# The first layer's lookup compares on VectorE, written with a scalar operand

## The chip, the core and the metric

The kernel runs on one core of one Trainium2 chip. The metric is the device time of one execution in microseconds; medians of several executions are compared. On the core five engines work at the same time: TensorE (PE), VectorE (DVE), ScalarE (ACT), GpSimd (POOL) and SyncE (SP), which here only starts DMAs. They wait for each other through semaphores.

## What is computed

A graph network of four layers over 6250 nodes with 64 features and 200000 edges, sorted by their destination. Each layer normalizes the nodes' features (h), gathers h at each edge's source node, makes a message of it and sums the messages at the destination. The four layers differ in the message; the change concerns the first:

```python
h = jnp.maximum(_layernorm(x, axis=-1), 0.0)
msg = jnp.concatenate([h[src], edge_attr_32], axis=1)            # 64 + 32 features
agg = jax.ops.segment_sum(msg, dst, num_segments=h.shape[0])
x = x + relu(jnp.concatenate([h, agg], axis=1) @ W.T + b)
```

The second and the fourth layer have attention over the edges of a destination (a softmax of scores), the third a weighted sum.

## The kernel before

**Tiling.** The edges, padded, form 1568 tiles of 128, and four tiles are a batch: 392 batches of 512 edges. Each layer is one pass over all batches, one instruction stream per engine, written with a helper `pipeline` (L160): in step t an engine works through a list of stages, each for batch t minus the stage's lag. The first layer's pass is `sum_sweep` (L916, called as "sum0" in L1782). The second layer's pass is `score_sweep`, the third's `kept_sum_sweep`, the fourth's `attention_sweep`.

**Rows by gather.** GpSimd fetches the source nodes' rows from HBM, one indirect DMA per tile of 128 edges (L781, in `gather_stage`), so four per batch, each with 128 node numbers that lie in `idx_slots`. A ring of 8 batches of row buffers (`sum_rows`, a view of `rows`) receives them; before a batch's gathers GpSimd waits until TensorE's sum of eight batches ago is done. The other passes gather too, but the third reads stored rows.

**Rows by lookup.** One batch in eight (the fourth of a block of eight) is not gathered but looked up. For it, the one-hot matrix of source node against edge is built in 49 pieces: piece n has a one where an edge's source is node 128 n + lane. The 512 source numbers of the batch, as int16 and the same in all 128 lanes, stand in `look_lines` (a view of `pre`). VectorE compares them with the lane's node number for pieces 0 to 31 (stage `hots`, four instructions per batch, L1178), into a ring of four tiles `dve_hots` (a view of `dst_pairs`, under whose name the rows show it). ScalarE makes pieces 32 to 48 with Square and Relu (L1075, L1079). TensorE multiplies each piece with the node features, split into three bf16 parts (L1105), and VectorE sums the result into the row buffer once per block (`fill`, L1192). So 48 blocks have 32 compares each: 1536.

**The lane's node number.** `node_at` (float32, 128 lanes x 32, L300) holds 128 n + lane, made by an iota at the start (L550). `node_pairs` (int16, 128 x 32 x 2, L302) is the same number twice over, copied from it (L558).

**The rest of the pass.** VectorE's stages in their order are: `build` (L1136, a one-hot of the destinations), the first compare, `low` (L1156), the second compare, `high` (L1163), the third compare, `add` (L1146, which takes the sum of the batch six steps before from TensorE), the fourth compare, `fill`. The constant operands of `build`, `low` and `high` lie in PSUM (`iota_mark` and `lane_mark`, in a bank); the compares of `hots` have both operands in SBUF. TensorE per batch: the sum, eight float32 matrix instructions (L1097), then the lookups of six or seven pieces. SyncE loads edge data and lines once in four batches, stores 712 KB for the third layer's pass with them, and loads `look_lines` and `idx_slots` once in eight.

**The scalar form elsewhere.** The second and the fourth layer's passes have one compare per batch of 512 int16 numbers with a number per lane, bf16 out, with the scalar `window_lane` (float32, one per lane), in `hot_stage` (L861).

Of the kernel before, what the change touches and what calls it, by code (L numbers as in the profile page):

```python
# [33 lines left out]
ALU = mybir.AluOpType  # L34
# [3 lines left out]
P = 128  # L38
# [10 lines left out]
BATCH = TILES_PER_BATCH * P  # L49
# [84 lines left out]
def landed(eng, sems, b, per_use):  # L134

    ring = len(sems)
    eng.wait_ge(sems[b.slot(ring)], (b.uses(ring) + 1) * per_use)
# [100 lines left out]
def graph_layers(nc, a, out):  # L238
    ctx = contextlib.ExitStack()
    with ctx:  # L240
        def sb(name, shape, dt=F32):
            return ctx.enter_context(nc.sbuf_tensor(name, shape, dt))
# [57 lines left out]
        node_at = sb("node_at", [P, HOTS_DVE])  # L300
        lane_pair = sb("lane_pair", [P, 1, 2], BF16)
        node_pairs = sb("node_pairs", [P, HOTS_DVE, 2], I16)  # L302
# [613 lines left out]
        def sum_sweep(name):  # L916
# [4 lines left out]
            def sweep():  # L921
                with Phase(nc, name) as ph:
# [8 lines left out]
                    s_hot_dve, s_used_dve, s_square, s_hot_act, s_used_act, s_filled = (  # L931
                        ph.sem(n) for n in ("hot_dve", "used_dve", "square", "hot_act", "used_act",
                                            "filled"))
# [9 lines left out]
                    dve_hots, act_hots = hots_room[:, 0:4, :], hots_room[:, 4:6, :]  # L943
# [28 lines left out]
                    def block_of(b):  # L972
                        return b.uses(LOOK_EVERY)

                    def has_lookup(b):
                        return b.i is not None or b.off < N_BATCHES - LOOK_EVERY

                    def look_in(b):
                        return look_lines[:, b.of_group(LOOK_EVERY).slot(2), :]

                    def hots_dve(b):
                        n = HOTS_DVE // LOOK_EVERY
                        return range(n * b.slot(LOOK_EVERY), n * (b.slot(LOOK_EVERY) + 1))
# [148 lines left out]
                    def _(dve):  # L1132
# [35 lines left out]
                        def hots(b, which):  # L1168
                            if not has_lookup(b):
                                return  # L1170
                            if b.slot(LOOK_EVERY) == 0 and which == 0:
                                landed(dve, s_look, b.of_group(LOOK_EVERY), 16)
                            before = block_of(b) * HOTS_DVE
                            for n in hots_dve(b)[which:which + 1]:
                                if n >= 4 or not b.early(LOOK_EVERY):
                                    dve.wait_ge(s_used_dve, before + n - 3)
                                wide = [P, BATCH // 2, 2]
                                dve.tensor_tensor(  # L1178
                                    dve_hots[:, n % 4, :].rearrange("p (e t) -> p e t", t=2),
                                    look_in(b).rearrange("p (e t) -> p e t", t=2),  # L1180
                                    node_pairs[:, n:n + 1, :].to_broadcast(wide),
                                    ALU.is_equal).then_inc(s_hot_dve, 1)

                        def fill(b):
                            if b.slot(LOOK_EVERY) != LOOK_EVERY - 1 or not has_lookup(b):
# [12 lines left out]
                        for tiles in src_groups:  # L1198
                            value = of_tiles(normed, tiles)
                            left = parts_left.rearrange("p (j d) -> p j d", d=D)[:, 0:len(tiles), :]  # L1200
                            parts = [parts_of(tiles)[:, :, n, :] for n in range(PARTS)]
                            c.do(split(dve, c, value, left, parts))
                        hot0, hot1, hot2, hot3 = (functools.partial(hots, which=n) for n in range(4))
                        dve.wait_ge(s_marks, 2)
                        pipeline(dve, [(0, build), (6, hot0), (2, low), (6, hot1), (2, high),
# [1124 lines left out]
```

## Time and profile before

| | us |
|---|---|
| median of 3 runs | 6827.51 |
| lowest and highest | 6827.16, 6832.52 |
| the profiled execution | 6814.61 |
| its span in the profile | 6812.8 |

The profile is of one execution. In its rows a line begins with the line number of the kernel, the engine, the operation and what is written and read, by the names of the buffers. "Busy" is the time in which an engine has an instruction in work; instructions of one engine can overlap at their ends. "Idle before" is the time in which the engine was idle ahead of the group's instructions, with what ended it; "issue" there is time in which it waited for nothing that the profile shows. PEclk, or the number behind the counts in the rows by window, is TensorE's granted clock as a share of full speed.

### The profile page before, as it was taken

The numbers are of one execution on the slowest core, as the hardware profiler recorded it, in microseconds if no ns is written. First come the engines' busy times: TensorE is split into PE (matmuls) and PEld (weight loads), VectorE is DVE, ScalarE is ACT, GpSimd is POOL, SyncE is SP. The second block draws the span as 40 slices with busy tenths as digits, with TensorE's granted clock in tenths as the row PEclk, the third lists the DMA queues.
The fourth block names the chain that finished last, engine by engine and source line by source line (L and its number), as shares of the span: only waits on it lengthen the run. The fifth ranks groups of instructions, "written<-read, shape, count | busy, mean of one in ns | idle before, by whom it ended". The sixth has DMA issues, their size and how long they took to land. (4 is left out here: it accounts for less than half of the span.)

```text
span 6812.8 us, 161253 instructions
## 1 busy us (share of the span) xinstructions
PE 4834.9 (71%) x37998; PEld 3572.7 (52%) x38194; DVE 4807.6 (71%) x21264; ACT 4176.3 (61%) x11642; POOL 5060.7 (74%) x5713
## 2 busy tenths in 40 slices
PE   5777777777776666666665669998777777777774
PEld 4666767776662233322332258885555555555553
DVE  7666666666656666666666679997766666666667
ACT  4666666666625555555555569995566666666664
POOL 6777777777747777777777759994777777777774
PEclk8889888888877766677677679998777787777776
DMA  4333333333346666666666658886333333333231
GB/s 143 110 108 109 108 109 108 109 108 109 107 110 170 169 170 170 170 169 170 169 170 170 170 170 268 267 267 241 77 79 79 79 80 79 79 79 79 79 79 47
DMA packets 672779, 908.53 MB, mean 133 GB/s; under 512 B 141174, under 2 KB 429928, under 8 KB 672441
## 3 DMA queue, kind: packets, MB, share of 16 engines
q1 hardware_dynamic: 502366, 605.50, 29.0%
q0 software_dynamic: 168944, 301.30, 19.0%
q8 instruction: 42, 0.69, 0.0%
q10 hardware_dynamic: 1357, 0.47, 0.0%
q14 instruction: 70, 0.57, 0.0%
HBM read 696.57 MB, written 210.28 MB: 133 GB/s over the span
## 5 line engine op out<-in xcount | busy, mean ns | idle before, releaser
L781 POOL DMA_INDIRECT rows<-src_rows,idx_slots x1563 | 1494.9, 956 | 530.7 <-issue 475.2
L781 POOL DMA_INDIRECT rows<-rel_rows,idx_slots x1563 | 1481.9, 948 | 509.8 <-issue 447.7
L781 POOL DMA_INDIRECT rows<-node_rows,idx_slots x1371 | 1423.4, 1038 | 439.7 <-issue 410.2
L1371 PE MATMUL bank<-onehot,ones 128*128 128x512 f32 x1568 | 1235.5, 882 | 130.0 <-ACT onehot L1380 123.4
L1380 ACT ACTIVATE onehot<-ident,fresh_slots 128x128 f32<-128x128 f32 x3136 | 989.3, 386 | 35.6 <-DVE fresh_slots L1507 33.9
L1075 ACT ACTIVATE dst_pairs<-pre,minus_node 128x512 bf16<-128x512 int16 x816 | 580.6, 717 | 664.9 <-PE bank L1105 664.7
L1468 PE MATMUL bank<-w_e,edge_in 128*128 128x256 f32 x784 | 400.3, 606 | 751.4 <-DVE onehots L861 726.8
L1451 ACT ACTIVATE onehot<-onehots,exp_bias 128x512 bf16<-128x512 f32 x392 | 283.0, 722 | 936.4 <-DVE max_by_chunk L1549 889.8
L1468 PEld LDWEIGHTS bank<-w_e,edge_in 128*128 128x128 f32 x784 | 167.3, 264 | 1245.0 <-DVE onehots L861 801.5
L1105 PE MATMUL bank<-by_chunk,dst_pairs 128*128 128x192 bf16 x6144 | 725.6, 267 | 9.3 <-DVE dst_pairs L1178 9.2
L1178 DVE TENSOR_TENSOR dst_pairs<-pre,node_pairs 128x512 bf16<-128x512 int16 x1536 | 631.9, 411 | 0.0
L1105 PEld LDWEIGHTS bank<-by_chunk,dst_pairs 128*128 128x128 bf16 x6144 | 592.9, 107 | 34.7 <-DVE dst_pairs L1178 14.8
L1674 PE MATMUL bank<-rows,onehot 128*128 128x65 f32 x3136 | 539.8, 327 | 55.8 <-DVE wide_room L1767 53.8
L1492 DVE TENSOR_TENSOR pre<-bank,rows 128x256 f32<-128x256 f32 x392 | 166.0, 423 | 569.7 <-DMA rows<-src_rows,idx_slots 566.1
L1079 ACT ACTIVATE dst_pairs<-dst_pairs,ones 128x512 bf16<-128x512 bf16 x816 | 540.8, 707 | 1.6
L1674 PEld LDWEIGHTS bank<-rows,onehot 128*128 128x128 f32 x3136 | 496.8, 241 | 72.0 <-issue 61.7
L1146 DVE TENSOR_TENSOR wide_room<-bank,wide_room 96x128 f32 x392 | 111.4, 284 | 597.0 <-PE bank L1097 595.9
L1629 ACT ACTIVATE onehot<-onehots,edge_in 128x128 f32<-128x128 bf16 x1568 | 500.7, 390 | 20.0
L1299 ACT ACTIVATE onehot<-onehots,edge_scale 128x128 f32<-128x128 bf16 x1568 | 500.9, 390 | 14.6 <-DVE onehots L1354 14.5
L1690 DVE CUSTOM_DVE_ANT_0 pre<-bank,rows 128x64 f32<-128x64 f32 x1568 | 258.8, 221 | 319.8 <-DMA rows<-rel_rows,idx_slots 315.4
L1614 ACT ACTIVATE shrink<-grown 128x1 f32<-128x1 f32 x392 | 79.5, 203 | 648.7 <-DVE grown L1718 648.7
L1105 PE MATMUL bank<-wide_room,dst_pairs 128*128 128x192 bf16 x3264 | 439.7, 261 | 24.8 <-ACT dst_pairs L1079 24.7
(306 smaller groups left out, 11964.5 us busy)
## 6 DMA issues: line engine op xcount, KB each, us to landing
edge_in<-dst_line SPq DMA_DIRECT2D x392, 256.0 KB
spill<-rows SPq DMA_DIRECT2D x392, 256.0 KB
rows<-spill SPq DMA_DIRECT2D x392, 256.0 KB, 3.2
hot_rows<-rows SPq DMA_DIRECT2D x98, 712.0 KB
onehots<-hot_rows SPq DMA_DIRECT2D x196, 356.0 KB, 3.5
onehots<-src_low SPq DMA_DIRECT2D x98, 512.0 KB, 6.3
edge_in<-in_ea_l SPq DMA_DIRECT2D x98, 256.0 KB
edge_in<-in_eaT_l SPq DMA_DIRECT2D x392, 64.0 KB
```

The source lines that it names most:

```text
L781: pool.indirect_dma_start(out=to[:, b.slot(ROW_RING), g, :], out_offset=None, in_=table, in_offset=bass.IndirectOffsetOnAxis(ap=idx_slots[ ...
L1075: act.activation(act_hots[:, n % 2, :], look_in(b), ACT.Square, bias=minus_node[:, n:n + 1]).then_inc(s_square, 1)
L1079: act.activation(act_hots[:, n % 2, :], act_hots[:, n % 2, :], ACT.Relu, scale=-1.0, bias=ones[:, 0:1])\
L1105: last = pe.matmul(look_banks(b)[g // 2][:, at:at + PARTS * D], hot[:, g * P:(g + 1) * P], node_parts(j), start=(j == 0 and g % 2 == 0), s ...
L1178: dve.tensor_tensor(dve_hots[:, n % 4, :].rearrange("p (e t) -> p e t", t=2), look_in(b).rearrange("p (e t) -> p e t", t=2), node_pairs[:, ...
L1299: last = act.activation(onehot[:, b.slot(RING), g, :], plain_of(b)[:, g, :], ACT.Copy, scale=edge_scale[:, b.slot(RING), g:g + 1])
L1371: return pe.matmul(bank, ones[:, :], diag[:, b.slot(2), :, :].rearrange("p g e -> p (g e)"), start=start, stop=True)
L1380: last = act.activation(diag[:, b.slot(2), g, :], ident[:, :], ACT.Copy, scale=fresh_slots[:, b.slot(2 * RING), g:g + 1])
L1451: act.activation(exp_out, masked1[:, b.slot(2), :], ACT.Exp, bias=exp_bias[:, slot, :], accum_out=exp_sum[:, slot, :])
L1468: pe.matmul(to, edge_blocks[:, b.slot(RING), :], w1_e[:, :, :].rearrange("p g f -> p (g f)"), start=True, stop=False)
L1629: last = act.activation(weighted[:, b.slot(2), g, :], onehot_b[:, b.slot(ONEHOT_RING), g, :], ACT.Copy, scale=share[:, b.slot(RING), g:g + 1])
L1674: last = pe.matmul(summed, weighted[:, b.slot(2), g, :], rows[:, b.slot(ROW_RING), g, D:2 * D + 1], start=(g == 0), stop=(g == TILES_PER_B ...
```

## The change

The four compares of `hots` per batch were tensor-tensor instructions over pairs of elements: the numbers of `look_lines`, seen as 256 pairs, against the pair in `node_pairs`, which is read again for each of the 256. They become tensor-with-scalar instructions: the 512 numbers against one float32 scalar per lane, column n of `node_at`. Output, waits, semaphores and place in the order are the same; each engine has as many instructions as before. `node_pairs` stays in the program and is read by nobody.

```diff
                             for n in hots_dve(b)[which:which + 1]:
                                 if n >= 4 or not b.early(LOOK_EVERY):
                                     dve.wait_ge(s_used_dve, before + n - 3)
-                                wide = [P, BATCH // 2, 2]
-                                dve.tensor_tensor(
-                                    dve_hots[:, n % 4, :].rearrange("p (e t) -> p e t", t=2),
-                                    look_in(b).rearrange("p (e t) -> p e t", t=2),
-                                    node_pairs[:, n:n + 1, :].to_broadcast(wide),
-                                    ALU.is_equal).then_inc(s_hot_dve, 1)
+                                dve.tensor_scalar(dve_hots[:, n % 4, :], look_in(b),
+                                                  node_at[:, n:n + 1], None, ALU.is_equal)\
+                                   .then_inc(s_hot_dve, 1)
```

## Rows read from the trace of the kernel before

**Rows 1.** The page's head: the span, and each engine's busy time, share, instructions.

```profile
span 6812.8 us, 161253 instructions
PE 4834.9 (71%) x37998; PEld 3572.7 (52%) x38194; DVE 4807.6 (71%) x21264; ACT 4176.3 (61%) x11642; POOL 5060.7 (74%) x5713
```

**Rows 2.** Costliest groups, whole execution: GpSimd's gathers. Busy us, mean ns | idle before, releasers.

```profile
L781 POOL DMA_INDIRECT rows<-src_rows,idx_slots x1563 | 1494.9, 956 | 530.7 <-issue 475.2
L781 POOL DMA_INDIRECT rows<-rel_rows,idx_slots x1563 | 1481.9, 948 | 509.8 <-issue 447.7
L781 POOL DMA_INDIRECT rows<-node_rows,idx_slots x1371 | 1423.4, 1038 | 439.7 <-issue 410.2
```

**Rows 3.** Single lines, whole execution: duration ns min/median/max, first and last start.

```profile
L781 POOL DMA_INDIRECT rows<-src_rows,idx_slots x1563: 942/946/2442, 1973.6 to 3943.4; - x196
L781 POOL DMA_INDIRECT rows<-rel_rows,idx_slots x1563: 940/944/2438, 4765.2 to 6724.8; - x196
L781 POOL DMA_INDIRECT rows<-node_rows,idx_slots x1371: 940/945/2167, 61.1 to 1901.0; - x196
L1178 DVE TENSOR_TENSOR dst_pairs<-pre,node_pairs x1536: 403/411/489, 82.0 to 1877.0; 128x512 bf16<-128x512 int16 x192
```

**Rows 4.** Waits, 500 to 1900 us: who waited for whom, us, times, longest.

```profile
DVE wide_room L1146 <- PE bank L1097: 455.6, 172, 7.2
PE bank L1097 <- DMA rows<-node_rows,idx_slots: 111.1, 35, 5.2
POOL rows L781 <- PE bank L1097: 5.5, 18, 0.3
```

**Rows 5.** Windows: stretch, length, busy us and count by engine, clock, DMA, GB/s.

```profile
500.00:1900.00 1400.00, 1049.32 (x9591) 971.79 (x9589) 939.64 (x2438) 875.93 (x1544) 1081.82 (x1045) 0.88 0.39 108
...
1200.00:1205.00 5.00, 2.98 (x24) 2.39 (x21) 2.48 (x7) 3.36 (x6) 3.78 (x5) 0.83 0.98 281
1205.00:1210.00 5.00, 4.09 (x23) 3.92 (x24) 1.94 (x5) 1.15 (x4) 3.78 (x5) 0.51 0.20 45
1215.00:1220.00 5.00, 5.00 (x57) 4.74 (x56) 5.00 (x15) 4.84 (x10) 3.99 (x4) 1.00 0.18 44
```

**Rows 6.** Timeline, first pass: start us, us, engine, line; gathers, then compares.

```profile
1202.06 1.24 POOL L781 DMA_INDIRECT rows<-node_rows,idx_slots  x1 [0.30 <-issue]
...
1237.90 1.13 POOL L781 DMA_INDIRECT rows<-node_rows,idx_slots  x1 [0.30 <-issue]
...
1202.07 0.41 DVE L1178 TENSOR_TENSOR dst_pairs<-pre,node_pairs 128x512 bf16<-128x512 int16 x1
...
1237.80 0.41 DVE L1178 TENSOR_TENSOR dst_pairs<-pre,node_pairs 128x512 bf16<-128x512 int16 x1
```

**Rows 7.** Groups, GpSimd, 1880 to 1902 us.

```profile
L781 POOL DMA_INDIRECT rows<-node_rows,idx_slots x18 | 17.0, 945 | 5.5 <-issue 4.6 <-DMA rows<-node_rows,idx_slots 0.6 <-PE bank L1097 0.3
```

**Rows 8.** Groups, VectorE, 500 to 1900 us: the compares, and the adds.

```profile
L1178 DVE TENSOR_TENSOR dst_pairs<-pre,node_pairs 128x512 bf16<-128x512 int16 x1175 | 483.3, 411 | 0.0
L1146 DVE TENSOR_TENSOR wide_room<-bank,wide_room 96x128 f32 x299 | 85.0, 284 | 456.6 <-PE bank L1097 455.6
```

**Rows 9.** The later passes' compares, single line, whole execution, as in rows 3.

```profile
L861 DVE TENSOR_SCALAR onehots<-edge_in,window_lane x784: 336/345/573, 2000.6 to 6727.4; 128x512 bf16<-128x512 int16 x196
```

**Rows 10.** Groups, GpSimd: 2200 to 3900 us (second layer), 5000 to 6400 us (last).

```profile
L781 POOL DMA_INDIRECT rows<-src_rows,idx_slots x1352 | 1289.7, 954 | 411.8 <-issue 411.8
...
L781 POOL DMA_INDIRECT rows<-rel_rows,idx_slots x1121 | 1059.5, 945 | 341.6 <-issue 321.8 <-PE bank L1674 19.8
```

**Rows 11.** Timeline, last layer's pass: gathers, then compares.

```profile
5022.39 1.05 POOL L781 DMA_INDIRECT rows<-rel_rows,idx_slots  x1 [0.30 <-PE bank L1674]
...
5472.43 0.94 POOL L781 DMA_INDIRECT rows<-rel_rows,idx_slots  x1 [0.30 <-issue]
...
5022.29 0.34 DVE L861 TENSOR_SCALAR onehots<-edge_in,window_lane 128x512 bf16<-128x512 int16 x1
...
5472.41 0.35 DVE L861 TENSOR_SCALAR onehots<-edge_in,window_lane 128x512 bf16<-128x512 int16 x1
```

## The prediction

> **What bounds the kernel now.** The execution spans 6812.8 us, and no engine is busy for more than three quarters of it [rows 1], so the bound has to be read pass by pass. I first took the costliest groups of instructions of the whole execution, GpSimd's alone [rows 2]. The first layer's pass issues 1371 gathers. They are busy 1423.4 us, and between them lie 410.2 us that are called issue, 0.30 us ahead of each one. The sum, 1833.6 us, fills the pass: its first gather starts at 61.1 us and its last at 1901.0 us [rows 3], which is 1840 us. So GpSimd does nothing but issue gathers there, one behind the other, and hardly waits for anybody. The list of waits says the same for the stretch from 500 to 1900 us [rows 4]: GpSimd waits 5.5 us for TensorE's sums (the wait that makes a row buffer free), while VectorE waits 455.6 us for those sums and TensorE waits 111.1 us for gathered rows. The busy time of the engines in that stretch [rows 5]: TensorE 1049 us of 1400, VectorE 940, ScalarE 876, GpSimd 1082, and its 0.30 us per gather beside it make 1396. The pass therefore takes gathers times their period, now 1.038 + 0.30 us. The compares that the change touches are VectorE work, and VectorE is idle for a third of the pass. Of its own time nothing counts.
>
> **What a gather pays for the compares.** A gather of this pass takes 1038 ns in the mean, but its median is 945 ns and its shortest 940 [rows 2, 3]. The long ones can be read one by one [rows 6]. The gather at 1202.06 us, with a compare starting 0.01 us after it, takes 1.24 us, and the one at 1237.90 us, with one that started 0.10 us before it, takes 1.13 us. The compares themselves take 0.41 us either way; it is the gather that yields. Behind the last compare (at 1877.0 us [rows 3]) the other VectorE work of the pass goes on, and 18 gathers of 18 take 945 ns in the mean [rows 7]. So the excess of 1038 - 945 = 93 ns per gather, 127 us over 1371 gathers, comes with these compares. There are 1536 of them, 1.12 per gather, so one costs GpSimd 83 ns.
>
> **The change part by part.** It takes 1536 tensor-tensor compares of 411 ns [rows 8] and puts as many tensor-with-scalar compares in their places. Same input, same output, same waits and same order; the second operand is now a float32 number per lane, which is not streamed. No DMA, semaphore or loop changes.
>
> *VectorE's own time.* The later passes have just this form: 128x512, bf16 from int16, with a float32 number per lane as the scalar, 784 times, 345 ns in the median [rows 9]. That is 411 - 345 = 66 ns less, times 1536 = 101 us of VectorE time. All of it lies beside GpSimd's row of gathers, in an engine that waits a third of the time: 0 us. If that cover were gone (were VectorE the bound), it would be a gain of 101 us more; nothing shows that.
>
> *GpSimd's gathers.* This is the whole sum: 1371 gathers times the part of the 93 ns that goes. What the new form costs a gather is bounded by the two passes that have it once in four gathers. In the last layer gathers take 945 ns in the mean of a long stretch, with a median of 944: 1 ns each, 4 ns per compare [rows 3, 10]. In the second layer they take 954 ns, with a median of 946: 8 ns each, 32 ns per compare, if all of it is put on this form, though that pass has other VectorE instructions with two operands in the same memory [rows 3, 10]. With 1.12 compares per gather these make 4 to 36 ns of excess per gather. I take the value in between from single gathers of the last layer [rows 11]. One that starts 0.10 us behind such a compare takes 1.05 us, 0.11 us more than its like: it is let go 0.10 + 0.11 = 0.21 us after the compare's start. The old form lets go of the gather at 1237.90 us after 0.10 + 0.19 = 0.29 us, and where it starts together with a gather it wins and costs that 0.30 us [rows 6]. The new form, starting 0.02 us ahead of a gather, costs it nothing (0.94 us, the compare 0.35 us). So the stretch of unlucky starts shrinks from about 0.3 us (all starts up to 0.29 us ahead of the gather, or with it) to about 0.12 us (from 0.21 to some 0.09 us ahead), and the mean delay in it from half of 0.30 us to half of 0.12 us. The price falls to (0.12 x 0.06) / (0.3 x 0.15) = 16% of 83 ns, 13 ns per compare, 15 ns per gather; these are estimates from the few gathers shown. The rest, 93 - 15 = 78 ns times 1371, is a gain of 107 us, rounded up to 108. The ends: at 4 ns of excess, and even a little below nothing if all gathers came to the shortest one's 940 ns, 98 x 1371 = 134 us; at 36 ns of excess, 57 x 1371 = 78 us; with the 40 ns per compare (45 per gather) that the second layer's whole pass gives (956 - 946, times 4 [rows 2, 3]), 48 x 1371 = 66 us.
>
> *What comes late next.* The batch period falls from 4.68 us (1400 us over 299 batches, counted by VectorE's adds [rows 8]) to about 4.40 us. TensorE is idle 351 us of these 1400, 1.17 us per batch, so it can give the 0.28 us. Its work is not smooth: in the five microseconds from 1200 us the DMA engines are at 0.98 and TensorE waits for rows, in the next five its granted clock is 0.51 (of its two levels the lower, 1.2 GHz), and from 1215 us it is at 1.00 and 5.00 of 5 us busy [rows 5]. It is catching up there on rows that have piled up while GpSimd went on; that the rows pile up and GpSimd never waits is why this doesn't bound the pass. Price: 0.
>
> The sum: 6814.6 us of the profiled execution (6812.8 us of span [rows 1] and 1.8 us around it) - 108 = 6706.6 us. The median of the runs shown stands 12.9 us above that execution, so against it 6827.5 - 108 = 6719.5 us.
>
> **The rivals.**
>
> *Contention by length.* The new compare also keeps GpSimd away, for as long as it runs. The excess then falls only with the record, 345 of 411 ns: 127 x 66 / 411 = 20 us, so 6807.5 us. For it: a compare that reads two streams and one that reads a single stream twice as fast may use the same wires. Against it: gathers in the last layer, whose excess is 1 ns where this would give 83 x 345 / 411 / 4 = 17 ns. The Trainium skill (GPSIMD Engine Reference, "Key points") says that GpSimd shares its SBUF interfaces with VectorE and that there is contention both with instructions that have two SBUF inputs and with those in a 2-port mode; VectorE: DVE Perf Modes, "The perf-mode tier table", lets a 16-bit tensor-with-scalar instruction run in the mode with both ports. By that rule the change swaps one offender for another, and this rival is what it would give; the trace agrees that both forms delay a gather, but not that they do so alike.
>
> *TensorE and its stalls take over.* If the stalls behind each burst of DMA are fixed and TensorE is already as late as GpSimd, the pass stays as long as it is: 6827 us. For it: TensorE has no idle time outside these stalls, and each is followed by a stretch at half clock. Against it: then GpSimd would wait for free row buffers, and it waits 5.5 us in 1400 [rows 4].
>
> *The engines lock into the bad phase* (slower). VectorE follows TensorE, TensorE follows the rows, the rows follow GpSimd; the starts could settle so that nearly each gather comes 0.1 us behind a compare. At 0.11 to 0.13 us per gather that is 151 to 178 us in place of the 127 of today: 24 to 51 us slower, 6865 us at mid-price, and it decides once more than some 70 to 85% of all gathers are hit. Against it: with 1.12 compares per gather and a stretch of 0.12 us in a period of 1.25 us, a tenth is hit at random.
>
> **How the numbers follow.** The forecast has 0.82, by-length contention 0.06, TensorE's takeover 0.08 (some of it between), the bad phase 0.04. The forecast's own span is 6827.5 - 134 = 6693 us to 6827.5 - 66 = 6761 us. I widen the upper end to 6780 us for the 13 us between executions and for a takeover in part; what lies beyond it is the rest of the rivals. A measurement here can tell 0.2%, 14 us, from no change. Faster: the forecast, by-length contention and a small part of the takeover, 0.89; same 0.07; slower 0.04.
>
> **What the profile after would show.** Right: gathers of the first pass at 950 to 965 ns in the mean, 0.30 us of issue each as before, GpSimd still without waits for TensorE's sums; the new compares at 345 ns; the pass about 108 us shorter, all later passes as long as before. Gathers at 1020 ns or more say contention by length or the bad phase; few gathers of 1.2 us but many of 1.05 us would be the latter. Gathers at 950 ns and GpSimd waiting for the sums would be TensorE's takeover. What would make the forecast wrong before all of these is a compare that takes other than 345 ns here, since its hold on the gathers is read from that form.

## The result, and the profile after

| | before, us | after, us |
|---|---|---|
| median | 6827.34 | 6717.59 |
| lowest to highest | 6823.07 to 6832.52 | 6716.24 to 6724.61 |
| executions | 4 | 4 |
| span of the profiled execution | 6812.8 | 6716.2 |

The ratio after to before is 0.9841, with a 95% interval of 0.9824 to 0.9858: 110 us faster. In a later session on the same kind of chip the two stood at 6715.63 to 6824.03 us, 0.9845 (0.9828 to 0.9861).

The head of the changed kernel's page, which answers [rows 1], and GpSimd's gathers in its part on groups (busy us, mean ns of one, idle before), which answer [rows 2]:

```profile
span 6716.2 us, 161448 instructions
PE 4876.0 (73%) x38193; PEld 3558.2 (53%) x38194; DVE 4737.8 (71%) x21264; ACT 4170.5 (62%) x11642; POOL 4968.3 (74%) x5713
```

```profile
L781 POOL DMA_INDIRECT rows<-src_rows,idx_slots x1563 | 1499.1, 959 | 530.5 <-issue 475.6
L781 POOL DMA_INDIRECT rows<-rel_rows,idx_slots x1563 | 1484.5, 950 | 510.1 <-issue 444.5
L781 POOL DMA_INDIRECT rows<-node_rows,idx_slots x1371 | 1322.1, 964 | 439.6 <-issue 404.4
```

The first pass's gathers (`node_rows`) went from 1038 to 964 ns in the mean, from 1423.4 to 1322.1 us in all: 101 us. The idle time ahead of them is the same to 0.1 us (439.7 and 439.6). The gathers of the second and the last layer's passes are 3 and 2 ns longer, which gives back 7 us of GpSimd's time there. VectorE's busy time fell by 70 us, 4807.6 to 4737.8.

Single lines of the changed kernel, as in [rows 3] (min/median/max ns, first and last start). The compares of `hots` are now L1177.

```profile
L781 POOL DMA_INDIRECT rows<-src_rows,idx_slots x1563: 942/949/2442, 1871.7 to 3846.0; - x196
L781 POOL DMA_INDIRECT rows<-rel_rows,idx_slots x1563: 939/947/2442, 4666.5 to 6628.9; - x196
L781 POOL DMA_INDIRECT rows<-node_rows,idx_slots x1371: 941/947/1415, 60.7 to 1799.6; - x196
L1177 DVE TENSOR_SCALAR dst_pairs<-pre,node_at x1536: 333/341/550, 82.4 to 1774.8; 128x512 bf16<-128x512 int16 x192
```

The pass runs from 60.7 to 1799.6 us, 1739 us; before it was 1840 [rows 3]: 101 us shorter, where the span is shorter by 97. The longest gather of the pass is now 1415 ns, where it was 2167.

Waits from 500 to 1780 us (who waited for whom, us, times, longest), which answer [rows 4], and the window of the same stretch, which answers [rows 5]:

```profile
DVE wide_room L1146 <- PE bank L1097: 415.5, 147, 7.1
PE bank L1097 <- DMA rows<-node_rows,idx_slots: 139.3, 37, 4.8
POOL rows L781 <- PE bank L1097: 8.8, 29, 0.3
```

```profile
500.00:1780.00 1280.00, 987.83 (x9368) 923.68 (x9368) 859.59 (x2375) 854.35 (x1513) 972.01 (x1011) 0.89 0.41 115
```

GpSimd waits 8.8 us for the sums in 1280; it is still the bound. VectorE still waits 415 us.

### The profile page after: what moved, and what is told of

Same layout as the page of the kernel before. It is cut to its first block and busy times, and to the rows that moved or that the text cites. A ratio compares the mean times of both kernels' runs of the same rounds, so it can differ in the third digit from the quotient of the medians.

```text
span 6716.2 us, 161448 instructions
## 1 busy us (share of the span) xinstructions
PE 4876.0 (73%) x38193; PEld 3558.2 (53%) x38194; DVE 4737.8 (71%) x21264; ACT 4170.5 (62%) x11642; POOL 4968.3 (74%) x5713
## 5 line engine op out<-in xcount | busy, mean ns | idle before, releaser
L781 POOL DMA_INDIRECT rows<-node_rows,idx_slots x1371 | 1322.1, 964 | 439.6 <-issue 404.4
L1105 PE MATMUL bank<-by_chunk,dst_pairs 128*128 128x192 bf16 x6144 | 710.1, 264 | 5.3 <-DVE dst_pairs L1177 5.3
L1177 DVE TENSOR_SCALAR dst_pairs<-pre,node_at 128x512 bf16<-128x512 int16 x1536 | 553.0, 360 | 0.0
```

The source lines that it names most:

```text
L781: pool.indirect_dma_start(out=to[:, b.slot(ROW_RING), g, :], out_offset=None, in_=table, in_offset=bass.IndirectOffsetOnAxis(ap=idx_slots[ ...
L1105: last = pe.matmul(look_banks(b)[g // 2][:, at:at + PARTS * D], hot[:, g * P:(g + 1) * P], node_parts(j), start=(j == 0 and g % 2 == 0), s ...
L1177: dve.tensor_scalar(dve_hots[:, n % 4, :], look_in(b), node_at[:, n:n + 1], None, ALU.is_equal)\
```

## The experiments

All of them change the first layer's pass only. "Gathers" is the mean duration of its 1371 gathers, in the whole profiled execution; each experiment is compared with runs of the kernel before on its own chip in its own session, so the ratio counts and not the microseconds.

| kernel | compares 1, 2, 3, 4 of a batch | gathers, ns | median, before beside it, us | ratio (95%) |
|---|---|---|---|---|
| before | old, old, old, old | 1038 | | 1 |
| changed | new, new, new, new | 964 | 6717.59, 6827.34 | 0.9841 (0.9824 to 0.9858) |
| e1 | old, new, old, new | 973 | 6720.77, 6814.16 | 0.9862 (0.9845 to 0.9878) |
| e2 | old, PSUM, old, PSUM | 984 | 6739.59, 6814.16 | 0.9887 (0.9871 to 0.9904) |
| e3 | new, long, new, long | 1076 | 6865.84, 6814.16 | 1.0082 (1.0065 to 1.0098) |
| e4 | new, and a copy beside | 974 | 6726.88, 6814.16 | 0.9873 (0.9857 to 0.9890) |
| e5 | new, two elements | 944 | 6685.12, 6816.02 | 0.9807 (0.9791 to 0.9823) |
| e6 | new, constant | 961 | 6708.41, 6816.02 | 0.9845 (0.9829 to 0.9862) |
| e7 | changed again | 966 | 6715.63, 6824.03 | 0.9845 (0.9828 to 0.9861) |
| e8 | old, new, old, old | 985 | 6745.57, 6824.03 | 0.9887 (0.9870 to 0.9903) |
| e9 | old, old, copy and old, old | 1024 | 6802.32, 6824.03 | 0.9969 (0.9957 to 0.9982) |
| e10 | old, old, old, new | 1024 | 6804.10, 6824.03 | 0.9969 (0.9957 to 0.9980) |

**The time is the gathers' length.** Over this table the median moves with the gathers: e3's 112 ns more than the changed kernel's, times 1371, are 154 us, and the ratios lie 0.0241 apart, 164 us. From e5 to before it is 94 ns, 129 us, and 131 us were measured. So the length of the gathers explains the time, and what follows is about what sets it.

### e4: is it VectorE's own time?

```diff
+                                if which == 3:
+                                    if not b.early(1):
+                                        dve.wait_ge(s_pad, b.v)
+                                    dve.tensor_copy(banks[3][:, 0:P], iota_mark).then_inc(s_pad, 1)
```

> The changed kernel with one more VectorE instruction per batch, a copy of 128 numbers per lane from PSUM to PSUM (about 270 ns, what four new compares save against four old ones). My theory (VectorE's own time lies beside GpSimd's gathers): 6718 us as the changed kernel, gathers at 964 ns. Rival (the gain was VectorE's 101 us): about 6820 us.

The group of the gathers, whole execution (busy us, mean ns | idle before):

```profile
L781 POOL DMA_INDIRECT rows<-node_rows,idx_slots x1371 | 1335.0, 974 | 439.4 <-issue 406.5 <-DMA idx_slots<-in_src_l 21.9 <-PE bank L1098 10.7
```

Nearly all of the gain is still there with the copy in: 0.9873, where 0.9841 to 0.9845 was measured without it. The 0.3% that it costs are 19 to 22 us, and the gathers show 10 ns more each, 14 us. So VectorE's own time is not the gain. But the gathers became longer with a copy that reads and writes PSUM alone. That was not expected. By the measure that is explained under e1, over the whole pass, the compares of the first place now cost a gather 55 ns for 36 in the changed kernel, and those of the second 16 for 5, in the same form. It was the first sign that what counts is also when the compares start, and not their form alone.

### e2, e3: what about a compare holds a gather?

In e2 the second and the fourth compare have their node numbers in PSUM, with one operand left in SBUF; in e3 they have both in SBUF, one element at a time.

```diff
+                    node_mark = banks[2][:, 2 * P:2 * P + HOTS_DVE]
...
+                                if n % 2:
+                                    dve.tensor_tensor(
+                                        dve_hots[:, n % 4, :], look_in(b),
+                                        node_mark[:, n:n + 1].to_broadcast([P, BATCH]),
+                                        ALU.is_equal).then_inc(s_hot_dve, 1)
```

```diff
+                                if n % 2:
+                                    dve.tensor_tensor(
+                                        dve_hots[:, n % 4, :], look_in(b),
+                                        node_at[:, n:n + 1].to_broadcast([P, BATCH]),
+                                        ALU.is_equal).then_inc(s_hot_dve, 1)
```

> The first and the third compare of a batch in the old form; the second and the fourth as a tensor-tensor compare whose node numbers lie in PSUM, as those of the neighbouring stages do, so that it has one operand in SBUF only. It runs longer, about 680 ns as its neighbours, for 411. My theory (two operands in SBUF are what holds the gather): the longer compare costs a gather nothing, 945 + 46 = 991 ns, about 6764 us, as long as the 0.54 us per batch that VectorE has more find room in its idle time. Rival (a gather is held by any compare while it runs, by its length): 83 x 680 / 411 = 137 ns for the long ones, gathers at 945 + 46 + 77 = 1068 ns, about 6869 us.

The gathers of the whole execution, and the compares with numbers in PSUM from 500 to 1780 us:

```profile
L781 POOL DMA_INDIRECT rows<-node_rows,idx_slots x1371 | 1348.9, 984 | 439.7 <-issue 407.2 <-DMA idx_slots<-in_src_l 22.2 <-PE bank L1099 10.1
...
L1180 DVE TENSOR_TENSOR dst_pairs<-pre,bank 128x512 bf16<-128x512 int16 x566 | 379.8, 671 | 0.0
```

> The first and the third compare in the new form; the second and the fourth as a tensor-tensor compare with both operands in SBUF that takes one element at a time (float32 node number, read over and over), about 680 ns for the 411 of the old form. My theory (a gather that starts within the streaming waits for its end, so the price goes with the square of the length of streaming, 0.55 us for 0.30): 83 x 3.4 = 280 ns per long compare, gathers at 945 + 157 + 10 = 1112 ns, about 6920 us. Rival, price by length alone: 137 ns per long one, 1032 ns, about 6811 us. Rival, a fixed price per instruction with two operands in SBUF: 1001 ns, 6770 us.

The same for e3, with its long compares:

```profile
L781 POOL DMA_INDIRECT rows<-node_rows,idx_slots x1371 | 1475.7, 1076 | 439.8 <-issue 412.0 <-DMA idx_slots<-in_src_l 22.2 <-PE bank L1097 5.2
...
L1178 DVE TENSOR_TENSOR dst_pairs<-pre,node_at 128x512 bf16<-128x512 int16 x528 | 357.2, 676 | 0.0
```

The two compares take the same 671 and 676 ns of VectorE and differ in where the second operand lies. With it in PSUM the gathers are at 984 ns (expected 991 by two operands in SBUF, 1068 by length); with it in SBUF at 1076. The two kernels also differ in their first and third compares: e2 has the old form there and e3 the new one, so that this difference works against e2, and 984 against 1076 is no measure of one operand. The places of the edit alone give one (the measure is explained under e1; whole pass): the second and the fourth compare cost 2 and 0 ns in e2, and 144 and 95 ns in e3. And single gathers say it: of 185 in e2 and e11 in which the only compare was one with numbers in PSUM, started at most 0.6 us before the gather or with it, none took over 10 ns more than 945; in e3 such a compare with both operands in SBUF let go of its gather 0.55 us after its own start, 22 times of 22. A compare of 0.67 us costs a gather nothing unless both its operands lie in SBUF. This is shown. That 984 came near the 991 is no support for the 83 ns per old compare on which the 991 was built, as e1 tells. How the price grows with length is less so: 1112 was expected by the square and 1032 by the length, and 1076 lies between them.

### e5, e6: streaming, or the scalar?

```diff
-                                dve.tensor_scalar(dve_hots[:, n % 4, :], look_in(b),
+                                dve.tensor_scalar(dve_hots[:, n % 4, 0:2], look_in(b)[:, 0:2],
```

```diff
-                                                  node_at[:, n:n + 1], None, ALU.is_equal)\
+                                                  float(n * P), None, ALU.is_equal)\
```

> The changed kernel with each compare cut to the first two of its 512 elements; the one-hot pieces are left as they were before, so the looked-up rows are not computed. What is left of the compares is their fixed part. My theory: a gather is held by the streaming alone; gathers at 945 ns, 19 less than the 964 of the changed kernel, 26 us in all, about 6692 us. Rival (what is left of the excess comes from the instruction's start, above all from fetching the scalar operand): gathers stay at about 960 ns, 6712 us.

```profile
L781 POOL DMA_INDIRECT rows<-node_rows,idx_slots x1371 | 1294.2, 944 | 439.4 <-issue 405.3 <-DMA idx_slots<-in_src_l 21.8 <-PE bank L1097 12.2
...
L1177 DVE TENSOR_SCALAR dst_pairs<-pre,node_at x1536: 211/219/482, 82.3 to 1746.8; 128x2 bf16<-128x2 int16 x192
```

> The changed kernel with a constant (128 n) in the instruction in place of the lane's number from memory, so the one-hot pieces are wrong for all lanes but the first. The streaming is the same. My theory: the record shortens by what fetching the scalar takes, to about 280 ns, and gathers stay at 960 to 965 ns, 6715 us. Rival (fetching the scalar holds gathers as well): gathers at 950 ns, about 6698 us.

```profile
L781 POOL DMA_INDIRECT rows<-node_rows,idx_slots x1371 | 1318.2, 961 | 439.7 <-issue 406.2 <-DMA idx_slots<-in_src_l 22.2 <-PE bank L1097 11.0
...
L1177 DVE TENSOR_SCALAR dst_pairs<-pre x1536: 274/279/456, 82.1 to 1773.2; 128x512 bf16<-128x512 int16 x192
```

(Each fence: the gathers of the whole execution, then the compare's single line, min/median/max.) Cut to two elements the compare still takes 219 ns of 341, yet the gathers are at 944 ns, the length without any compare [rows 7]. With a constant it takes 279 ns, and the gathers stay at 961. So the rest of the excess, 964 against 945 ns, comes with the streaming of the 512 elements and not with the fetch of the scalar; 20 ns per gather, 27 us, is all that is left in it.

### e1: half of the old form

```diff
+                                if n % 2:
+                                    dve.tensor_scalar(dve_hots[:, n % 4, :], look_in(b),
+                                                      node_at[:, n:n + 1], None, ALU.is_equal)\
+                                       .then_inc(s_hot_dve, 1)
+                                else:
...
```

> Two of the four compares per batch (the second and the fourth) in the new form, the first and the third in the old one. My theory: a gather pays for each compare by its form, some 83 ns per old one and some 17 ns per new one (the 964 ns of the changed kernel against 945), 0.56 of each per gather: gathers at 945 + 46 + 10 = 1001 ns, about 6770 us, halfway. Rival (VectorE's and GpSimd's starts lock, so that the form hardly counts): a jump to one of the ends, 964 or 1038 ns.

```profile
L781 POOL DMA_INDIRECT rows<-node_rows,idx_slots x1371 | 1333.6, 973 | 439.3 <-issue 409.5 <-DMA idx_slots<-in_src_l 21.9 <-PE bank L1097 7.3
```

My theory gave 1001 ns, and 973 came, nearer to the rival's jump to 964: two old compares of four cost 9 ns more than none. The price per compare on which the sum was built, 83 ns, isn't a constant. To see where it falls, I went through the timeline compare by compare. For each place in the batch the table gives how much longer than 945 ns the gathers were that began from 0.15 us before to 0.31 us behind the compare's start, per compare, and in brackets how many of the compares had a gather starting within 0.03 us of them, and how many of those gathers took over 1.1 us. It was worked out from the rows of the timeline of the two engines, 258 to 335 batches each, of which examples stand below. A gather is counted where it starts; if a later compare lengthens it once more, that stands in the column of the earlier one.

```
ns per compare          first        second       third            fourth
before                  68 (13, 12)  38 (28, 27)  175 (141, 135)   43 (12, 12)
changed                 31 (13, 5)    4 (3, 0)      4 (96, 0)      18 (19, 11)
e1 old new old new      63 (9, 7)    11 (51, 10)   10 (112, 0)     18 (10, 9)
e8 old new old old      56 (9, 9)    20 (20, 17)    9 (89, 0)      50 (10, 6)
e10 old old old new     67 (7, 5)    18 (30, 13)  169 (136, 135)   21 (11, 8)
e9 old, copy ahead of 3 55 (4, 4)    59 (32, 28)  116 (1, 1)       33 (10, 10)
```

Before, more than half of the price sat on gathers that started at the third compare. In 141 of 335 batches a gather started within 0.03 us of it, where chance would give some 15 (0.06 us of a period of 1.34 us), and 135 of these gathers were held. In e1 that same third compare, in its old form, had 112 such meetings, and not one gather was held over 1.1 us.

The reason for the meetings is in the timeline of the kernel before (start us, us, engine; gathers first, then the first and the third compare of one batch):

```profile
357.25 1.17 POOL L781 DMA_INDIRECT rows<-node_rows,idx_slots  x1 [0.30 <-issue]
358.73 1.23 POOL L781 DMA_INDIRECT rows<-node_rows,idx_slots  x1 [0.31 <-issue]
...
357.19 0.41 DVE L1178 TENSOR_TENSOR dst_pairs<-pre,node_pairs 128x512 bf16<-128x512 int16 x1
358.73 0.41 DVE L1178 TENSOR_TENSOR dst_pairs<-pre,node_pairs 128x512 bf16<-128x512 int16 x1
```

The first compare holds the gather until 357.19 + 0.29 = 357.48 us. From there this gather takes its 0.94 us and the issue 0.30 us, so the next begins some 1.54 us behind the compare's start. The third compare begins 1.54 us behind the first as well (within 0.01 us in nearly all batches). All 131 gathers that a first compare had held were followed by one that began within 0.02 us of the third compare, and that one was on average 0.375 us too long. The two engines were in step by the sum of their durations.

### e8, e9, e10: the step, taken apart

```diff
e8:  +                                if which == 1:      (new form, else the old one)
e10: +                                if which == 3:      (new form, else the old one)
e9, in the kernel before:
+                                if which == 2:
+                                    if not b.early(1):
+                                        dve.wait_ge(s_pad, b.v)
+                                    dve.tensor_copy(banks[3][:, 0:P // 2], iota_mark[:, 0:P // 2])\
+                                       .then_inc(s_pad, 1)
```

> The changed kernel itself, as the reference for the runs beside it on the same chip. Every theory: 0.984 of the kernel before, gathers of the first pass at 964 ns.

> Only the second of the four compares per batch in the new form. Price by form alone: the gain is what the second compare costs, about 34 ns per batch by the gathers that begin while it runs (38 ns in the old form, 4 in the new): gathers at 1028 ns, 13 us faster than before. My new theory (resonance): before, a gather that the first compare held is followed, 1.54 us after that compare's start, by the next gather, and the third compare starts 1.54 us after the first as well, so the two meet to within 10 ns and the gather loses 0.3 us and more. A shorter second compare brings the third to 1.47 us, and the meeting is decided for the gather or does not happen: the third compare's 175 ns per batch fall below 40, gathers at about 980 to 990 ns, 65 to 80 us faster than before.

```profile
L781 POOL DMA_INDIRECT rows<-node_rows,idx_slots x1371 | 1350.5, 985 | 439.4 <-issue 408.1 <-DMA idx_slots<-in_src_l 21.8 <-PE bank L1097 9.1
```

One compare of four in the new form brings 53 of the 74 ns, at 985 ns, where its own price was at most 38 ns per batch, 11 ns per gather: the time fell by 78 us where price by form gave 13. The third compare, unchanged, fell from 175 to 9 ns. A batch of e8 (gathers, then the first and the third compare; both of these in the old form, L1183):

```profile
467.38 1.13 POOL L781 DMA_INDIRECT rows<-node_rows,idx_slots  x1 [0.30 <-issue]
468.82 0.94 POOL L781 DMA_INDIRECT rows<-node_rows,idx_slots  x1 [0.30 <-issue]
...
467.28 0.41 DVE L1183 TENSOR_TENSOR dst_pairs<-pre,node_pairs 128x512 bf16<-128x512 int16 x1
468.82 0.46 DVE L1183 TENSOR_TENSOR dst_pairs<-pre,node_pairs 128x512 bf16<-128x512 int16 x1
```

The first compare holds its gather as before, and the next gather and the third compare meet again at 468.82 us. But now the gather takes 0.94 us, and it is the compare that is longer, 0.46 us for 0.41. The second compare is 0.07 us shorter, so the third could begin 1.47 us behind the first (the median of all batches); in these meetings it begins 1.54 us behind. It seems to have been due first and to have waited for the gather.

> Only the fourth compare per batch in the new form; it stands behind VectorE's wait for the sum and leaves the distance from the first to the third compare as it was. Resonance: the third compare stays in step with the gathers, 1.54 us, and goes on costing some 175 ns per batch; only the fourth's own 12 ns per batch go: gathers at 1035 ns, 5 us faster than before. Rival (one compare of the new form anywhere brings most of the gain, as two of four did): 980 to 1000 ns, 50 us or more faster.

```profile
L781 POOL DMA_INDIRECT rows<-node_rows,idx_slots x1371 | 1403.9, 1024 | 439.4 <-issue 410.9 <-DMA idx_slots<-in_src_l 21.8 <-PE bank L1097 6.7
```

```profile
428.38 1.09 POOL L781 DMA_INDIRECT rows<-node_rows,idx_slots  x1 [0.31 <-issue]
429.78 1.24 POOL L781 DMA_INDIRECT rows<-node_rows,idx_slots  x1 [0.30 <-issue]
...
428.24 0.41 DVE L1183 TENSOR_TENSOR dst_pairs<-pre,node_pairs 128x512 bf16<-128x512 int16 x1
429.78 0.41 DVE L1183 TENSOR_TENSOR dst_pairs<-pre,node_pairs 128x512 bf16<-128x512 int16 x1
```

The fourth compare does not lie between the first and the third, and the third went on losing: 169 ns, 135 of 136. The gathers are at 1024 ns, 11 less than expected, and the time fell by 20 us where 5 were expected. By the table the fourth compare gave 22 ns per batch, where I had put 12, and the second 20 ns although it is unchanged; with 3.5 gathers per batch these are 12 ns per gather. Why the second one became cheaper is open.

The 175 and the 169 ns of the third are not the same thing, though. When VectorE doesn't have to wait for the sum, the fourth compare starts 0.53 us behind the third, while the gather that the third held is still running. The same place in the kernel before and in e10 (gather, third compare, fourth compare):

```profile
497.21 1.78 POOL L781 DMA_INDIRECT rows<-node_rows,idx_slots  x1 [0.30 <-PE bank L1097]
...
497.22 0.41 DVE L1178 TENSOR_TENSOR dst_pairs<-pre,node_pairs 128x512 bf16<-128x512 int16 x1
497.75 0.41 DVE L1178 TENSOR_TENSOR dst_pairs<-pre,node_pairs 128x512 bf16<-128x512 int16 x1
```

```profile
423.91 1.23 POOL L781 DMA_INDIRECT rows<-node_rows,idx_slots  x1 [0.31 <-issue]
...
423.91 0.41 DVE L1183 TENSOR_TENSOR dst_pairs<-pre,node_pairs 128x512 bf16<-128x512 int16 x1
424.44 0.34 DVE L1178 TENSOR_SCALAR dst_pairs<-pre,node_at 128x512 bf16<-128x512 int16 x1
```

Before, in 57 of the 141 meetings the fourth compare started within the gather, and these gathers lost 505 ns in the mean; the other 84 lost 274. In e10, where the fourth has the new form, it was 68 of 136, and they lost 297 ns against 291. So an old-form compare can lengthen a gather that is half done, too, and some 34 of the third's 175 ns per batch (57 times 208 over 345 batches) belonged to the fourth. The gain of e10 does not show in the third's column because the meetings became more frequent, 136 in 258 batches for 141 in some 340. Why they did is open.

> The kernel before, all four compares in the old form, with one more VectorE instruction per batch in front of the third compare: a copy of 64 numbers per lane from PSUM to PSUM, which puts the third compare some 0.15 us later (1.69 us after the first for 1.54). Price by form alone: as before, 1038 ns and no gain, or a little slower. Resonance: the third compare's 175 ns per batch fall to the 30 to 60 of the others, gathers at 1000 ns, about 50 us faster than before, although VectorE has more to do.

```profile
L781 POOL DMA_INDIRECT rows<-node_rows,idx_slots x1371 | 1403.9, 1024 | 439.4 <-issue 408.7 <-DMA idx_slots<-in_src_l 21.8 <-PE bank L1098 8.5
```

Moved by 0.13 us, with nothing else changed, the third compare met no gather any more (1 of 259), and the kernel before became 0.3% faster although it had one more instruction per batch. So the step is a cause by itself. But the gain was 14 ns where 38 were expected, and 116 of the 175 ns stayed. Some 41 of them lie on gathers that began 0.13 us before the third compare, some 73 on others that began about 0.18 us behind it and that it held. In both groups the loss is mostly that of the gathers in which the fourth compare started as well, as under e10: 90 gathers with 261 ns in the mean, 91 of the 116 ns, where 87 gathers without it lost 73 ns. Taking the third compare out of the meeting left the fourth where it was, 0.53 us behind the third. The price depends on the place within 0.1 us, and two points do not draw that curve.

### e11, e12: the best of both, and a session in which nothing was gained

e11 has the first and the fourth compare with node numbers in PSUM and the other two in the new form; e12 is the changed kernel beside it.

```diff
+                                if which in (0, 3):
+                                    dve.tensor_tensor(
+                                        dve_hots[:, n % 4, :], look_in(b),
+                                        node_mark[:, n:n + 1].to_broadcast([P, BATCH]),
+                                        ALU.is_equal).then_inc(s_hot_dve, 1)
```

> The first and the fourth compare, which in the changed kernel still cost GpSimd the most (31 and 18 ns each, by the gathers that begin around them, for 4 and 4 of the second and third), as tensor-tensor compares with the node numbers in PSUM (about 675 ns, costing a gather nothing where they were tried); the second and the third in the new form. Theory (price by form and place): gathers at 950 ns for 964, about 19 us below the changed kernel, as long as VectorE's additional 0.68 us per batch find room. Rival (VectorE then becomes late for TensorE's lookups, VectorE is busy for 3.7 of 4.4 us per batch): GpSimd begins to wait for the sums, and the time is that of the changed kernel or above.

> The changed kernel beside the mixed one on the same chip: 0.984 to 0.985 of the kernel before, gathers of the first pass at 964 to 966 ns.

The kernel before took 8611.71 us beside them, e11 8625.83 us (1.0023, 1.0009 to 1.0037) and the changed kernel 8617.26 us (1.0016, 1.0001 to 1.0031). All three were a quarter slower than in any other session, which I can't explain; in the changed kernel the second layer's gathers, which no experiment touches, waited 1198 us there for some 531. The gathers of e11 (group), then those of the changed kernel (group and single line, whole execution), and a window of its first pass:

```profile
L781 POOL DMA_INDIRECT rows<-node_rows,idx_slots x1371 | 1298.1, 947 | 1102.5 <-PE bank L1099 424.5
...
L781 POOL DMA_INDIRECT rows<-node_rows,idx_slots x1371 | 1303.9, 951 | 1083.8 <-PE bank L1097 398.1 <-issue 361.4 <-remote 302.4
...
L781 POOL DMA_INDIRECT rows<-node_rows,idx_slots x1371: 938/944/1346, 60.8 to 2425.6; - x196
...
100.00:1700.00 1600.00, 1013.31 (x8524) 903.75 (x8525) 792.71 (x2164) 789.16 (x1379) 876.63 (x922) 0.81 0.30 84
```

The gathers are short, 947 ns in the mean in e11, where 950 was expected, and 951 in the changed kernel, where 964 to 966 was. But the changed kernel's pass lasts 2365 us, since GpSimd waits 398 us in it for the sums and 302 us for something that the profile calls remote; in the window it is busy 877 us of 1600. What made the engines wait for each other longer is open. What the session does tell: where GpSimd waits, its gathers may get shorter and nothing is gained; the change, worth 110 us elsewhere, was worth nothing here. Whether e11 would beat the changed kernel on a chip that runs as the others did remains untried.

## Why the prediction was right, point by point

**The bound.** Right. GpSimd's gathers stood in one row before and after; the idle time ahead of them didn't move (439.7, 439.6 us), and in every session but the last all that changed the time changed their length. VectorE's 101 us counted for nothing directly (e4), as forecast; the 19 to 22 us that e4 cost came through the gathers.

**The cause.** Right that the gathers paid for these compares, and that a second operand read from SBUF element by element makes the difference: in the places that e2 and e3 changed, 2 and 0 ns against 144 and 95. Also right that streaming holds and not the rest of the instruction (e5, e6), and right in the two moments of release: in gathers that a single compare held (12 before, 8 after) they are 0.28 to 0.29 us behind the start of the old form (forecast 0.29) and 0.21 to 0.22 behind that of the new one (forecast 0.21).

**The excess after.** 945 + 15 = 960 ns forecast, 964 measured; 107 us forecast from it, 101 us measured in the pass and 110 us between the medians, against the 108 of the sum.

**The duration of the new compare.** 345 ns forecast, 341 in the median and 362 in the mean of the stretch. The mean shows what the forecast had seen in one pair only [rows 11]: the new form gives way. Its record was over 0.03 us longer than the median in nearly 40% of the second compares of a batch, and in 19% of the third.

**The price per compare.** Wrong, and hidden by a sum that came out. The step "one costs GpSimd 83 ns" spread 127 us evenly over 1536 compares, and the next one, "the stretch of unlucky starts", took starts as random. Neither holds: over half of the price lay on gathers that began at one compare in four, by a step of 1.54 us that both engines had, and part of it was the fourth compare lengthening the same gathers once more. The prediction's own figures were at odds there: at random a stretch of 0.3 us with a mean delay of 0.15 us in a period of 1.34 us gives 34 ns per old compare, not 83. With all four replaced the error does little, since the new form cost at most 31 ns in any place. With some replaced it does not cancel: the same working gave 1001 ns for e1 (973 came) and 13 us for e8 (78 came).

**The price of the new form.** 13 ns per compare forecast, 14 (the mean of the four in the table) to 17 (19 ns times 1371 over 1536) measured. That it fits is in part luck. Only the 16% came from single gathers; the 13 ns are 16% of the 83 that do not hold. The same stretch taken at random (0.12 times 0.06 us in 1.25 us) gives 6 ns, and with it the sum would have been 118 us and 6709 us. What carried the forecast was the 93 ns of excess, read from means and well measured: e5, in which the compares hardly stream, took all of it away.

**The rivals.** Contention by length is refuted by the result, 964 ns where it gave some 1023, and by e2 (984 ns, where it gave 1068). The page of the Trainium skill that was named for it (GPSIMD Engine Reference, "Key points") was right that both forms contend, since e5 takes 20 ns from the gathers of the new form, and silent on what decides here, how long each form holds a gather. TensorE's takeover did not come: GpSimd waited 8.8 us for the sums. The bad phase, put at 0.04 for the kernel after, would have needed 70 to 85% of the gathers hit. A milder lock was the state of the kernel before, where 505 of 1371 gathers were over 20 ns too long. That starts might lock had been thought of; that they might have done so already was not looked for, though the 2167 ns of the longest gather [rows 3] pointed at something other than a hold of 0.30 us: three compares started within it, and 82 gathers lost over 0.31 us each, together 44 of the 127 us.

## What to carry to other kernels

Where GpSimd's indirect DMAs are the bound, look at VectorE's instructions with both operands in SBUF: gathers of 1.24 us among many of 0.94 show them, and a scalar operand takes most of them away, one operand in PSUM, even at a longer duration, all. Before putting a price on each such instruction, group the gathers they hold by the instruction's place in the loop: two engines with fixed durations can be in step, and then one place can carry most of the price, an instruction shorter by 0.07 us elsewhere in the loop can remove it (e8), another shift can leave two thirds of it (e9), and half a change can bring nine tenths of the gain (e1).

## What the runs showed of the hardware that was not expected

A meeting of a gather and an old-form third compare to within 0.03 us went one way each time: in the kernel before 135 of 141 gathers were held, for some 0.3 us by the third alone, and in e1 and e8 none of 201 was, and there the compare was longer instead, 0.45 for 0.41 us. The difference lies in whether the compare was due at the same time (1.54 us behind the first) or 0.07 us earlier (1.47); why it then waits for the gather, rather than run ahead of it, the profile does not show.

The two engines exclude each other for parts of their instructions only. Old-form compares that started, as the only one, 0.12 to 0.45 us into a gather left it at 945 ns to within 16 ns (107 gathers before) and took their 0.41 us. Later in the gather the forms part. New-form compares took 0.34 us in the mean when they started in its first 0.45 us (440 of them), and 0.43 us, up to 0.55, when they started 0.5 to 0.7 us into it (264); old-form compares took 0.41 us at either place (412 and 204). What the gather does at that point is open.
